# Second context attention on the raw context: key and value weights folded into query and output weights, transposes in place of value products

## The reference

```python
kp = jnp.einsum('bsd,ed->bse', k, Wk)          # k = v = context (6404 x 128)
vp = jnp.einsum('bsd,ed->bse', v, Wv) + bv
qp = jnp.einsum('bsd,ed->bse', q, Wq) + bq     # q = x (1024 x 128)
scores = jnp.einsum('bqd,bkd->bqk', qp, kp) * scale
probs = jax.nn.softmax(scores, axis=-1)
ctx = jnp.einsum('bqk,bkd->bqd', probs, vp)
return jnp.einsum('bqd,ed->bqe', ctx, Wo) + bo
```

## Time and profile before

| what | us |
|---|---|
| median of 3 runs | 1976.42 (1976.32 to 1980.21) |
| the profiled execution | 1975.02 |
| its span in the trace | 1973.3 |
| the stretch of block 0's maxima, first tile on DVE to first scores on PE | 152.7 to 227.0 |

### The profile page before, as it was taken

How to read it: one execution, slowest core, us unless ns; L and a number is a source line. 1 busy time by engine, 2 the same in 40 slices (tenths; PEclk the granted TensorE clock), 3 DMA queues, 4 the chain that set the end, 5 groups by cost and what they waited for, 6 DMA issues and landing times. The chain is left out here.

```text
span 1973.3 us, 36573 instructions
## 1 busy us (share of the span) xinstructions
PE 1910.7 (97%) x14409; PEld 971.1 (49%) x14409; DVE 1514.5 (77%) x2805; ACT 1381.1 (70%) x2492; POOL 135.1 (7%) x115
## 2 busy tenths in 40 slices
PE   5999999999999999999999999999899999999997
PEld 2556644444444444444444444444344444777755
DVE  6878899999999999999999991333688855444334
ACT  5964688888888888888888888533488873444321
POOL 2850000000000000000000000000710000000000
PEclk8999999999999999999999999999899999999999
DMA  6210000000000000000000000132120000000000
GB/s 183 87 54 1 1 1 2 1 2 1 1 2 2 1 1 2 2 1 1 2 1 1 2 1 2 60 112 80 26 44 9 1 1 0 1 1 1 16 30 29
DMA packets 28022, 37.87 MB, mean 19 GB/s; under 512 B 7248, under 2 KB 21680, under 8 KB 27599
## 3 DMA queue, kind: packets, MB, share of 16 engines
q1 hardware_dynamic: 26670, 33.48, 6.1%
q10 hardware_dynamic: 1184, 2.10, 0.3%
HBM read 29.61 MB, written 0.65 MB: 15 GB/s over the span
## 5 line engine op out<-in xcount | busy, mean ns | idle before, releaser
L1157 DVE TENSOR_REDUCE sb_max_partial<-ps_max_ps 128x1 f32<-128x512 f32 (+1 forms) x1664 | 977.5, 663 | 42.9 <-PE ps_max_ps L893 41.8
L1139 ACT ACTIVATE sb_probs<-ps_score_ps 128x512 f32<-128x512 f32 (+1 forms) x1592 | 853.6, 597 | 108.0 <-PE ps_score_ps L1056 62.0
L1056 PE MATMUL ps_score_ps<-sb_q_stack,sb_key_stack 64*128 64x512 f32 x1561 | 566.0, 446 | 3.9 <-ACT sb_probs L1139 3.4
L893 PE MATMUL ps_max_ps<-sb_key_stack,sb_q_stack 64*128 64x512 f32 (+1 forms) x1560 | 555.6, 437 | 0.0
L1029 PE MATMUL ps_acc_ps<-sb_probs,sb_val_ones 128*32 128x256 f32 x6528 | 463.5, 387 | 0.2 <-ACT sb_probs L1139 0.2
L1056 PEld LDWEIGHTS ps_score_ps<-sb_q_stack,sb_key_stack 64*128 64x128 f32 x1561 | 265.0, 183 | 313.0 <-ACT sb_probs L1139 250.6
L893 PEld LDWEIGHTS ps_max_ps<-sb_key_stack,sb_q_stack 64*128 64x128 f32 x1560 | 264.9, 183 | 9.8 <-DVE sb_max_partial L1157 7.4
L1029 PEld LDWEIGHTS ps_acc_ps<-sb_probs,sb_val_ones 128*32 128x32 f32 x6528 | 157.0, 108 | 206.0 <-issue 131.9
L1860 DVE TENSOR_REDUCE sb_s_max_partial<-ps_s_ps 128x1 f32<-128x512 f32 x256 | 157.5, 683 | 27.8 <-PE ps_s_ps L1706 27.8
L1847 ACT ACTIVATE sb_s_probs<-ps_s_ps 128x512 f32<-128x512 f32 x256 | 141.0, 597 | 32.2 <-PE ps_s_ps L1734 23.7
L2094 DVE TENSOR_SCALAR_CACHE_REDUCE sb_x_scores<-ps_x_score_ps 128x1024 f32<-128x1024 f32 (+1 forms) x56 | 62.0, 1110 | 69.3 <-PE ps_x_score_ps L2081 69.3
(11 more groups left out here) (326 smaller groups left out, 1907.6 us busy)
## 6 DMA issues: line engine op xcount, KB each, us to landing
sb_val<-c_rows SPq DMA_DIRECT2D x16, 512.0 KB, 3.6
sb_e_gate_rows<-e_gate_dram SPq DMA_DIRECT2D x15, 512.0 KB, 4.1
sb_e_w<-L_ffn_rW SPq DMA_DIRECT2D x30, 128.0 KB, 2.1
sb_e_w<-L_ffn_W_T SPq DMA_DIRECT2D x24, 128.0 KB, 2.1
sb_ctx_T<-ctx_T SPq DMA_DIRECT2D x1, 1664.0 KB, 8.6
sb_ctx_T<-ctx_T ACTq DMA_DIRECT2D x1, 1538.0 KB, 9.6
sb_key_stack<-sb_key_halves SPq DMA_DIRECT2D x24, 64.0 KB, 2.3
sb_s_key_stack<-sb_s_highs SPq DMA_DIRECT2D x28, 32.0 KB
```

The source lines that it names most:

```text
L893: nc.tensor.matmul(bank((blk, u))[:, 0:n], queries, keys, start=True, stop=True).then_inc(tile_ready, 1)
L1056: nc.tensor.matmul(score_bank(blk, e), keys, queries, start=True, stop=True).then_inc(score_ready, 1)
L1139: nc.scalar.activation(probs[0:n, c % 3, j * HALF:(j + 1) * HALF], score_bank(blk, e)[0:n, :], ACT.Exp).then_inc(exp_done, 1)
L1157: nc.vector.tensor_reduce(partial[:, blk % 2, h, r:r + 1], bank((blk, u))[:, 0:RANGES[r][1]], AX.X, ALU.max).then_inc(tile_used, 1)
```

## The change

The weights are multiplied together once, so that the second context attention reads the context itself: the scores are `x (Wq^T Wk) ctx^T` with the query bias taken through `Wk`, and the output is `(probs ctx) (Wv^T Wo^T)`. The key jobs are gone. `ctx_T` is kept through layer 1 and takes the place of `key1_T`. `val1` gets the context turned to rows, so a value job is up to four transposes instead of four products. Two new jobs stand at places 0 and 2 of the list: one turns the three weight matrices, the other multiplies them (two products of 128 columns and one of one column); ACT copies both out. The list has 16 jobs instead of 27, so `jobs_at` sets one after every seventh tile (26, 33, ... 103) instead of about two in seven tiles. The scan stage gets a tile of its own for its working room. The last four jobs are the same value jobs as before.

```diff
 def lay_out(k):
-    k.key1_T = k.sb("key1_T", [P, CTX])
+    k.ctx_T = k.sb("ctx_T", [P, CTX])
     k.val1 = k.sb("val1", [P, NCH, D])
...
-    k.ctx_T = k.sb("ctx_T", [P, CTX], F32, k.layer0)
...
+        self.x1_w_q_k, self.x1_w_v_out, self.x1_b_q_k = k.sb("x1_w_q_k", [P, D]), k.sb("x1_w_v_out", [P, D]), k.sb("x1_b_q_k", [P, 1])
...
-        zs = k.key1_T[:, 0:2 * T].rearrange("p (s t) -> p s t", s=2)
-        conv = k.key1_T[:, 2 * T:4 * T].rearrange("p (s t) -> p s t", s=2)
-        dbc = k.key1_T[0:ROWS, 4 * T:5 * T]
+        scratch = k.sb("scratch", [P, 6 * T], F32, ctx)
+        zs = scratch[:, 0:2 * T].rearrange("p (s t) -> p s t", s=2)
+        conv = scratch[:, 2 * T:4 * T].rearrange("p (s t) -> p s t", s=2)
+        dbc = scratch[0:ROWS, 4 * T:5 * T]
...
-            key_jobs = [(c0, min(HALF, CTX - c0)) for c0 in range(0, CTX, HALF)]
             val_jobs = [(c, min(4, NCH - 1 - c)) for c in range(0, NCH - 1, 4)] + [(NCH - 1, 1)]
-            KEYS = len(key_jobs)
-            NJOBS = KEYS + len(val_jobs)
+            TURN_WEIGHTS, FOLD_WEIGHTS = 0, 2
+            turns_at = [i for i in range(len(val_jobs) + 2) if i not in (TURN_WEIGHTS, FOLD_WEIGHTS)]
+            turned_w = k.sb("x1_turned_w", [P, 3, D], F32, tmp)
+            NJOBS = len(val_jobs) + 2
...
             def layer1_job(pe, i, to):
-                if i < KEYS:
-                    c0, cols = key_jobs[i]
-                    ins = nc.tensor.matmul(to[:, 0:cols], k.wk1[:], k.ctx_T[:, c0:c0 + cols], start=True, stop=True)
+                if i == TURN_WEIGHTS:
+                    for j, w in enumerate((k.params.x1_w_q, k.wk1, k.wv1)):
+                        ins = nc.tensor.transpose(to[:, j * D:(j + 1) * D], w[:], k.ident[:])
+                elif i == FOLD_WEIGHTS:
+                    nc.tensor.matmul(to[:, 0:D], turned_w[:, 0, :], turned_w[:, 1, :], start=True, stop=True)
+                    nc.tensor.matmul(to[:, D:2 * D], turned_w[:, 2, :], k.params.x1_w_out[:], start=True, stop=True)
+                    ins = nc.tensor.matmul(to[:, 2 * D:2 * D + 1], turned_w[:, 1, :], k.params.x1_b_q[:], start=True, stop=True)
                 else:
-                    c, m = val_jobs[i - KEYS]
+                    c, m = val_jobs[turns_at.index(i)]
                     n = P if c < NCH - 1 else TAIL
                     for j in range(m):
-                        ins = nc.tensor.matmul(to[0:n, j * D:(j + 1) * D], k.ctx_T[:, (c + j) * P:(c + j) * P + n],
-                                               k.wv1[:], start=True, stop=True)
+                        ins = nc.tensor.transpose(to[0:n, j * D:(j + 1) * D], k.ctx_T[:, (c + j) * P:(c + j) * P + n], k.ident[:])
                 ins.then_inc(job_ready, 1)
...
             def copy_job(act, i, src):
                 act.wait_ge(job_ready, i + 1)
-                if i < KEYS:
-                    c0, cols = key_jobs[i]
-                    ins = nc.scalar.copy(k.key1_T[:, c0:c0 + cols], src[:, 0:cols])
+                if i == TURN_WEIGHTS:
+                    ins = nc.scalar.copy(turned_w[:], src[:, 0:3 * D].rearrange("p (j e) -> p j e", j=3))
+                elif i == FOLD_WEIGHTS:
+                    nc.scalar.copy(k.params.x1_w_q_k[:], src[:, 0:D])
+                    nc.scalar.copy(k.params.x1_w_v_out[:], src[:, D:2 * D])
+                    ins = nc.scalar.copy(k.params.x1_b_q_k[:], src[:, 2 * D:2 * D + 1])
                 else:
-                    c, m = val_jobs[i - KEYS]
+                    c, m = val_jobs[turns_at.index(i)]
...
-        w_q, b_q, w_out = k.params.x1_w_q, k.params.x1_b_q, k.params.x1_w_out
+        w_q, b_q, w_out, w_v_out = k.params.x1_w_q_k, k.params.x1_b_q_k, k.params.x1_w_out, k.params.x1_w_v_out
...
-                                       k.key1_T[:, i * HALF:i * HALF + n], start=True, stop=True)
+                                       k.ctx_T[:, i * HALF:i * HALF + n], start=True, stop=True)
...
-                    ins = nc.tensor.matmul(acc_ps[:, p % 2, (2 + s) * P:(3 + s) * P], acc_T[:, s * P:(s + 1) * P], w_out[:],
+                    ins = nc.tensor.matmul(acc_ps[:, p % 2, (2 + s) * P:(3 + s) * P], acc_T[:, s * P:(s + 1) * P], w_v_out[:],
```

More of the change, by code:

```diff
@@ L459, in state @@
             lo = (2 + m % RING) * T
-            return k.key1_T[:, lo:lo + T]
+            return scratch[:, lo:lo + T]
         w_kv = k.w_kv
```

## The result

The changed kernel takes 1967.83 us in the median of 4 runs (1967.57 to 1968.36), the kernel before 1978.32 beside it (4 runs, 1976.32 to 1980.94): a ratio of 0.9949, 95% interval 0.9937 to 0.9961. In a second group of runs on another chip it was 1967.69 against 1977.24, 0.9954 (0.9941 to 0.9968). The forecast was 1966.4 against 1976.42, a ratio of 0.9949.

What follows compares the result with a forecast made beforehand. PE was taken to bound tiles 20 to 103 of block 0's maxima, with DVE next; 9.4 us there plus 0.6 at the tail gave 10.0 us, so 1966.4 us against 1976.42, range 1964.0 to 1970.5 (8 in 10).

Steps and rivals of the forecast that it cites:

- The rival that the tiles wait for latency: Block 0's maxima: DVE's waits are query-product bursts that stay, so only 0.6 us is won, 1975.8 us; chance 0.05.
- the doubt drawn from the weight loads' share: Tiles 20 to 103: weight loads fill 76% of PE's time, below DVE's 87%, supporting the no-change rival; chance 0.05.
- PE's sum: Tiles 20 to 103: PE's work falls as 59.4 - 10.9 - 5.3 + 1.1 = 44.3 us.
- DVE's 49.4: Tiles 20 to 103: DVE needs 49.4 us for 84 tiles at 0.59 each, with small corrections, and becomes the later engine.
- The 0.5 us of stalls: Same tiles: allowance for folding, query and value products meeting on PE, as at tile 41; bounds 0 and 2 us.
- The tail's 0.6: After tile 103: PE turns the second shift sooner, winning 0.6 us before the first scores; bounds 0 and 0.75.
- The stretch with its tail: From tile 20 of block 0's maxima to the first scores: 9.4 + 0.6 = 10.0 us won.
- The copies and the renamed operands at nothing: ACT's 13 removed copies give nothing; the second context attention keeps shapes, counts and banks on the raw context.
- a granted clock of 0.5 inside the stretch: Named sign of being wrong: PE at half clock, 1.2 GHz, between tiles 20 and 103.
- the single dip that a rival put at some 1.7 us: Slower rival (0.04) called one 3.4 us half-clock dip at the tail likelier, costing some 1.7 us and leaving a gain.
- one later engine for the whole stretch: Tiles 20 to 103 priced as one sum, the later of PE's 44.3 and DVE's 49.4 us.
- 1.40 us from the profiled execution to the median: Whole kernel: the runs' median lies 1.40 us above the profiled execution, so 1965.0 becomes 1966.4 us.

Runs made afterwards that it cites:

- the pair with half the maxima: DVE reduces only 256 columns of each block 0 tile, in the changed kernel (1966.13 us) and in the kernel before (1978.05 us, 1977.89 unedited).
- the version with two held jobs: Changed kernel with two jobs held back instead of four, one job after every sixth tile, folding after tile 37: 1968.57 us against the changed kernel's 1967.69.
- the transposes alone: Kernel before with key jobs kept, value jobs as transposes and value weights folded into the output weights: 0.9971 of the kernel before, stretch 56.06 us.

## Why the prediction was right

*The bound.* PE before, DVE after: shown by the pair with half the maxima, in which DVE's work is worth 0.8 us in the one kernel and 5.1 in the other. The rival that the tiles wait for latency has fallen with it, and so has the doubt drawn from the weight loads' share (76% of the stretch): at that share PE was full and set the pace.

*The terms.* PE's sum, 44.3 us, measures 44.90 where DVE is no longer in its way. DVE's 49.4 measures 49.38 where the folding job does not meet a query product (two jobs held). The 0.5 us of stalls are 0.6, most of it at the one place that was named, tile 41; moving the folding job takes away half of that gap. The tail's 0.6 is 0.61. The stretch with its tail was to give 10.0 us and gave 9.99. PE's sum came so near with some luck: with DVE's work halved in both kernels PE's work falls by 13.7 us (58.57 to 44.90), while the terms take off 15.1; that the sum began at 59.4, 0.8 above the 58.57, made up for part of this. The gain did not hang on it, since DVE was the later one. One reading was wrong without harm: the first score waits for the copied jobs and the first half of the shift, not for both halves, as the version with two held jobs shows.

*The copies and the renamed operands at nothing.* ACT's busy time in the stretch fell from 23.5 to 17.6 us and nothing came of it; the second context attention kept its groups to 0.1 us in the first profiles (its 408 rows of weighing are passes, two to a product).

*The clock.* One of the signs that I had named for being wrong, a granted clock of 0.5 inside the stretch, came in one of two profiles of the changed kernel. It was the single dip that a rival put at some 1.7 us: it cost 1.5 and left the gain; I had put it at the tail, where it came once, in the version with two held jobs. The Trainium skill, in "TensorE: Matmul & The Clock Gate" (Part 4: PE-mode transpose), says that the full clock does not engage for transposes. Where they alternate with products this trace differs: in the second context attention 362 transposes run between products from 1661 to 1840 us, at a granted clock of 1.00 (the window for all engines, then for line 2128 alone: PE, PEld, clock, DMA).

```profile
1661.00:1840.00 179.00, 179.00 (x879) 131.86 (x878) 79.02 (x152) 73.01 (x136) 0.00 (x0) 1.00 0.00 1
...
1661.00:1840.00 179.00, 54.62 (x362) 45.00 (x362) 1.00 0.00 1
```

The spell in the stretch follows 3.4 us without a transpose, so no run here shows transposes lowering the clock. Nor is the opposite shown: the one profile with identity products in their place has no spell in the stretch, but neither have two of the four with transposes and the same pace.

*Where I was less right.* The sum's largest simplification, one later engine for the whole stretch, happened to hold with both parts of the change in and failed for the transposes alone by 1.4 us of the expected gain of 4.7 in the stretch. And 1.40 us from the profiled execution to the median was taken as fixed, while a second profile of the kernel before ended 2.8 us later, and the changed kernel's profiled execution, 1968.36 us where 1965.0 was forecast, lay above its median and not below. The forecast of the median is good to no better than that, and its nearness is in part luck.

## What to carry to other kernels

When two engines share a stretch, sum the work of each, take the later for every part of the stretch in which the mix stays the same, and stop the gain there: of the 14 to 15 us taken from the bound engine only 9.4 were won in the stretch. To know who sets a stretch, take work from the other engine and see whether it gets shorter. Compare stages, not two executions: in the kernel before the stretch repeated to 0.01 us while the ends of its two profiles lay 2.8 us apart.

## What the runs showed of the hardware that was not expected

PE's clock fell to 1.2 GHz (granted clock 0.50 and 0.51) inside the stretch in two of the four profiles with this pace and four held jobs (the changed kernel and the one with the folding job moved, two each), after 3.4 us in which PE's records covered 3.10 and 3.13 us. In the other two the same work covers 3.08 and 3.11 us, and the clock stays at 1.00; in the changed kernel's first profile:

```profile
183.51:186.91 3.40, 3.08 (x15) 2.08 (x14) 3.40 (x7) 0.57 (x1) 0.00 (x0) 1.00 0.00 0
186.91:190.31 3.40, 3.40 (x20) 2.71 (x20) 3.40 (x6) 1.76 (x3) 0.00 (x0) 1.00 0.00 0
```

So neither the order of the work nor the share that PE's records cover tells which of the two will follow; what decides it stays open. The Trainium skill, in "Perfetto Trace Analysis" (Identifying the Most-Contended Engine), calls that share no good measure of how near TensorE is to its peak. The pair with half the maxima agrees: PE's records cover 97% of the changed kernel's stretch, 48.66 of 49.98 us, and its work alone takes 44.90.
